# A memset of 128x384 on GpSimd between every two row scatters of a 64-expert routing group

## The reference, cut to what matters

```python
gates = jax.nn.softmax(logits, axis=-1)
w_topk, idx_topk = jax.lax.top_k(gates, TOPK)             # TOPK = 8
...
rank = jnp.arange(A) - starts[se]
valid = rank < CAPACITY                                   # CAPACITY = 160
buf = jnp.zeros((NUM_EXPERTS, CAPACITY, H), x.dtype).at[se, rank].set(x[st], mode='drop')
h = jnp.einsum('ech,efh->ecf', buf, expert_w1)
x1, x2 = jnp.split(h, 2, axis=-1)
out = jnp.einsum('ecf,ehf->ech', x1 * jax.nn.silu(x2), expert_w2)
```

## Time and profile before

| what | us |
|---|---|
| median of three timed runs | 3281.57 |
| lowest and highest of them | 3281.53, 3283.92 |
| span of the profiled execution | 3607.6 |
| TensorE busy in it | 2593.0 (72%) |
| VectorE busy | 2038.9 (57%) |
| GpSimd busy | 1846.4 (51%) |
| ScalarE busy | 1370.6 (38%) |
| scatters of line L1894, stage A | 160, 998 ns each |
| scatters of line L1894, stage B | 128, 977 ns each |

### The profile page before, as it was taken

How to read it: one execution, slowest core, us unless ns; L and a number is a source line. 1 busy time by engine, 2 the same in 40 slices (tenths; PEclk the granted TensorE clock), 3 DMA queues, 4 the chain that set the end, 5 groups by cost and what they waited for, 6 DMA issues and landing times. The chain is left out here.

```text
span 3607.6 us, 68811 instructions
## 1 busy us (share of the span) xinstructions
PE 2593.0 (72%) x24634; PEld 1681.5 (47%) x24634; DVE 2038.9 (57%) x5864; ACT 1370.6 (38%) x2937; POOL 1846.4 (51%) x2072
## 2 busy tenths in 40 slices
PE   1224994735499945689998899947388886999573
PEld 1113884423368834356555555536133332555362
DVE  4347334523443345547885587621699999787413
ACT  1111221301122222344665266622576763466323
POOL 5650775254317742126996213456488886123554
PEclk7666997856599977799999799978699999899786
DMA  9100896121019974331110101112221211111123
GB/s 373 48 1 8 213 224 155 45 66 31 27 41 226 226 191 108 138 120 21 19 19 3 20 19 30 48 55 56 102 94 48 94 62 40 22 20 35 43 80 92
DMA packets 222721, 294.13 MB, mean 82 GB/s; under 512 B 36704, under 2 KB 179583, under 8 KB 216288
## 3 DMA queue, kind: packets, MB, share of 16 engines
q1 hardware_dynamic: 172704, 249.85, 22.3%
q0 software_dynamic: 47616, 39.44, 5.8%
q10 hardware_dynamic: 2112, 1.05, 0.1%
HBM read 181.88 MB, written 107.12 MB: 80 GB/s over the span
## 5 line engine op out<-in xcount | busy, mean ns | idle before, releaser
L3783 POOL TENSOR_TENSOR l3am_db<-l3am_du,l3am_bs 128x1024 f32<-128x1024 f32 x127 | 298.0, 2367 | 39.9 <-DVE l3am_hh L4021 36.1
L4021 DVE TENSOR_TENSOR_SCAN l3am_hh<-l3am_dA,l3am_db 128x1024 f32<-128x1024 f32 x128 | 292.1, 2283 | 0.9 <-ACT l3am_dA L3921 0.7
L1217 POOL TENSOR_TENSOR l2a_pT<-l2a_pT,kept 128x512 int32<-128x512 int32 x213 | 265.1, 1280 | 45.4 <-ACT l2a_pT L1423 45.4
L3066 POOL DMA_INDIRECT l0f_table<-l0f2e_y,l0f2e_idx x128 | 178.9, 1398 | 177.1 <-DVE l0f2e_idx L3038 130.2
L3066 POOL DMA_INDIRECT l0f_table<-l0f1e_y,l0f1e_idx x128 | 179.6, 1403 | 139.2 <-DVE l0f1e_idx L3038 91.2
L4152 PE MATMUL l3am_y<-l3am_hc,ident 128*128 128x512 f32 x512 | 242.1, 596 | 0.0
L3921 ACT ACTIVATE l3am_dA<-l3am_dl,l3am_al 128x512 f32<-128x512 f32 x256 | 166.3, 682 | 130.8 <-DVE l3am_hh L4021 127.2
L1894 POOL DMA_INDIRECT l0f_rows<-l0f1r_row,l0f1r_idx x160 | 159.7, 998 | 103.1 <-issue 69.3
L1304 DVE CUSTOM_DVE_ANT_0 l2a_junk<-l2a_s,addend 128x256 f32<-128x256 f32 x486 | 178.1, 421 | 57.0 <-PE l2a_s L1540 44.6
L1297 DVE TENSOR_REDUCE l3f1a_mx<-l3f1a_s 128x2 f32<-128x512 f32 x243 | 156.5, 685 | 40.9 <-PE l3f1a_s L1540 32.4
L1297 DVE TENSOR_REDUCE l3f2a_mx<-l3f2a_s 128x2 f32<-128x512 f32 x243 | 156.4, 684 | 39.7 <-PE l3f2a_s L1540 32.1
(11 more groups left out here) (848 smaller groups left out, 7045.5 us busy)
## 6 DMA issues: line engine op xcount, KB each, us to landing
l3am_bs<-l3a_b SPq DMA_DIRECT2D x32, 1024.0 KB, 6.6
l0f1m_w<-in_L_ffn_expert_w SPq DMA_DIRECT2D x64, 384.0 KB
l0f2m_w<-in_L_ffn_expert_w SPq DMA_DIRECT2D x64, 384.0 KB
l1a_top<-l1a_kernel SPq DMA_DIRECT2D x16, 1024.0 KB, 12.6
l0f_rows<-blank SPq DMA_DIRECT2D x8, 1930.0 KB, 15.2
l0f1m_w<-in_L_ffn_expert_w SPq DMA_DIRECT2D x64, 192.0 KB
l0f2m_w<-in_L_ffn_expert_w SPq DMA_DIRECT2D x64, 192.0 KB
l3f_rows<-blank SPq DMA_DIRECT2D x8, 1440.0 KB, 11.6
```

Source lines behind the costliest of these rows:

```text
L1217: self.nc.gpsimd.tensor_tensor(t, t, self.kept[:, f // 8 % 2, :].unsqueeze(1).to_broadcast([P, 2, 2 * P]), ALU.mult).then_inc(self.cut_g, 1)
L3066: g.indirect_dma_start(out=tables[p], out_offset=bass.IndirectOffsetOnAxis(ap=idx[u % RING][:, a:a + 1], axis=0), in_=y[u % RING][:, a, :] ...
L3783: G.tensor_tensor(db[n % DB][:, :].rearrange("p (j t) -> p j t", j=CC), du[k % 2][:, :, :], bs[s // QUARTER][:, s % QUARTER, :].unsqueeze( ...
L4021: V.tensor_tensor_scan(hh[n % HH][:, :], dA[n % 2][:, :], db[n % DB][:, :], 0.0, ALU.mult, ALU.add).then_inc(h_ready, 1)
```

## The change

Between every two scatters of a group GpSimd sets a scratch tile of 128x384 floats to zero. A counting semaphore orders the memsets among themselves: each waits until the one before has ended, since they write the same tile. The scatters themselves wait for nothing new. The first scatter of a group has no memset ahead of it, so there are 31 to a group. In a group that is skipped the memsets are skipped too.

```diff
+    PAUSE = 384
...
+        self.pause = ph.sb("pause", [P, self.PAUSE])
...
+        self.paused = ph.sem("paused")
...
         for t in range(TPG):
             for j in range(self.K):
+                if t or j:
+                    k = n * (TPG * self.K - 1) + t * self.K + j - 1
+                    if k:
+                        g.wait_ge(self.paused, k)
+                    self.nc.gpsimd.memset(self.pause[:, :], 0.0).then_inc(self.paused, 1)
                 g.indirect_dma_start(out=self.m.rows, out_offset=bass.IndirectOffsetOnAxis(
                     ap=self.idx[u][:, t, j:j + 1], axis=0), in_=self.row[u][:, t, :], in_offset=None,
                     bounds_check=self.last_slot, oob_is_err=False).then_inc(sent, 16)
```

## The result

The changed kernel takes 3354.61 us (median of four runs, 3347.94 to 3360.22), the kernel before 3281.55 us: the ratio is 1.0221, 95% interval 1.0203 to 1.0239. The change makes it 73 us slower; the forecast was 110 us slower, 3392 us. The profiled execution of the changed kernel has a span of 3358.5 us, 1.7 us under its own time, where that of before had 3607.6 us against a median of 3281.6. So the two profiles differ by 249 us in the other direction than the times. That had to be understood first.

A forecast was written before the change was run, and what follows sets the result against it. GpSimd's string of scatters was taken to end the first routing stage and be about level with the other engines beside the attention; memsets add 64 + 46 = 110 us to 3281.6, giving 3392 us, range 3275 to 3425.

The forecast's parts named there:

- A: First routing stage (l0f1r), five groups of scatters: GpSimd ends it, so 155 memsets at 0.41 us add 64 us.
- B: Stage beside the block attention (l0a), four groups of scatters: 124 memsets add 51 us, of which 46 us count.
- The stall isn't in the runs to be predicted: Both scatter stages: engines stalled during back-to-back scatters mostly in the profiled execution, 326 us longer than the timed median.
- The accounting: Both scatter stages without stall: 108 us and 170 us less, together 278 us, close to the 326 us gap.
- The rest has no room: Outside the two scatter stages: no place for the 326 us, as TensorE is busy 46.5 of 50 us among experts.
- The price of a memset: Between two scatters on GpSimd: 0.14 + 0.41 + 0.16 - 0.30 = 0.41 us each, scatter pitch 1.70 us.
- The slack in B: Beside the block attention: GpSimd ends at 880 us, the other engines at 885, so 5 us of memsets are hidden.
- Rival 1: Both scatter stages: the stall is real in timed runs and memsets relieve it, 168 us faster, 3114 us; chance 0.13.
- Rival 2: Both scatter stages: scatters go out faster unprofiled, 1.0 us each, so some +35 us, 3317 us; chance 0.17.
- Rival 3: Between scatters: the memset runs in the existing gap, 14 us less slack, about 3290 us or no change; chance 0.09.
- Rival 4: Both scatter stages: the stall is real and memsets don't relieve it, 114 us slower, 3396 us; chance 0.09.
- rival 5: At each memset: the semaphore wait costs its high bound, 0.61 us each, 170 us in all, 3445 us; chance 0.07.

The follow-up runs named there:

- experiment 1: The kernel before, unchanged, timed and profiled again: 3281.41 us against 3281.69, ratio 1.0005.
- experiment 2: The changed kernel's memsets put in one stage only: first routing stage 3332.16 us, beside the block attention 3311.45 us, against 3281.69 for the kernel before.
- experiment 5: The changed kernel with memsets of 16 or 1024 elements in place of 384: 3602.99 and 3566.91 us, against 3605.6 for the kernel before on chip 3.
- experiment 9: The changed kernel, no edit, timed on chip 15: 3521.09 us against 3623.79 for the kernel before, ratio 0.9735.
- experiment 7: The changed kernel with 24 scatters that can't keep a row left out of the fifth group: 3321.95 us, ratio 1.0133 to the kernel before.

## Why the prediction was right, and where it wasn't

TensorE's first matmul on expert rows cuts the execution at the ends of A and B. By the tile view, in the kernel before on a stalled chip (first profile), before on a free one, changed on a free one, changed on a stalled one:

```profile
L2961 PE MATMUL l0f1e_x<-ident,l0f1e_row x128: 230/234/396, 354.4 to 578.0; 80*128 80x80 f32 x128
...
L2961 PE MATMUL l0f2e_x<-ident,l0f2e_row x128: 230/234/291, 1058.5 to 1279.4; 80*128 80x80 f32 x128
```
```profile
L2961 PE MATMUL l0f1e_x<-ident,l0f1e_row x128: 230/234/398, 254.5 to 481.4; 80*128 80x80 f32 x128
...
L2961 PE MATMUL l0f2e_x<-ident,l0f2e_row x128: 230/234/292, 802.5 to 1025.5; 80*128 80x80 f32 x128
```
```profile
L2969 PE MATMUL l0f1e_x<-ident,l0f1e_row x128: 230/234/392, 306.6 to 530.2; 80*128 80x80 f32 x128
...
L2969 PE MATMUL l0f2e_x<-ident,l0f2e_row x128: 230/234/396, 874.9 to 1099.0; 80*128 80x80 f32 x128
```
```profile
L2969 PE MATMUL l0f1e_x<-ident,l0f1e_row x128: 230/234/393, 305.1 to 530.6; 80*128 80x80 f32 x128
...
L2969 PE MATMUL l0f2e_x<-ident,l0f2e_row x128: 230/234/397, 960.5 to 1185.7; 80*128 80x80 f32 x128
```

| | to the first experts | from there to the second |
|---|---|---|
| before, stalled | 354.4 | 704.1 |
| before, free | 254.5 | 548.0 |
| changed, free | 306.6 (+52.1) | 568.3 (+20.3) |
| changed, stalled | 305.1 (-49.3) | 655.4 (-48.7) |

**The change on free chips** is 52 + 20 = 72 of the 73 us between the two spans. On stalled ones it is 49 + 49 = 98, for 92 us between the spans of these two profiles, which are of different chips; on chip 15 alone it is the measured 103. The stages behind have next to no part in it.

**The stall isn't in the runs to be predicted: right; that it belongs to the profiled execution: wrong.** "I conclude that the stall belongs mostly to the profiled execution" had the right consequence for the time, since the timed runs came from a free chip, but by all that the runs show the profile and the times were from two kinds of chips. That the sign came out right is luck to this extent: had the timed runs fallen where the profile did, the same change would have been some 100 us faster. The argument for the step was a sum, 278 us of stall against 326 us of difference, and a sum can't tell a profiler from a chip. In every run listed here the span is some 1.7 us shorter than the time of the same execution (3285.1 against 3286.84 in experiment 1). The Trainium skill ("Runtime: NRT & Kernel Launch", The ~15µs preamble/postamble breakdown) says that the profile's total is some 6 us longer than the execution time whatever the kernel; I had set its rule aside because of the 326 us. Its size and its direction aren't those of this case, 1.7 us the other way; its point, that the gap is small and steady, holds here. A gap of 326 us should have led me to look for two machines, not to the profiler.

**The accounting: good where it was worked out, wrong about the rest.** Without the stall A was to end at 241 against VectorE's 226: measured 247.6 and 227.9. The stall was put at 108 us in A and 170 in B: measured 99.9 and 156.1 (table). The 170 took 52.7 - 10.2 for each group, but the steps of the free chip alternate between some 11.7 and 10.2 us, and the groups fall on the longer ones; with 11.7 it is 4 x 41 = 164. "The rest has no room" failed: of the 322.5 us between the two profiles of before, some 70 lie from the first of the two 8-expert stages on. From the first matmul on queries and keys of the first one (L1540) to that of the second passed 3071.9 - 2032.9 = 1039.0 us on the stalled chip and 2786.7 - 1780.6 = 1006.1 on the free one, and from there to the end 535.7 and 498.4 us. Most of it, 31 and 27 us, is lost within the experts of these stages. TensorE's matmuls on the rows of the first, stalled and free (tile view):

```profile
L2961 PE MATMUL l3f1e_x<-ident,l3f1e_row x80: 272/273/447, 2395.0 to 2514.9; 128*128 128x128 f32 x80
```
```profile
L2961 PE MATMUL l3f1e_x<-ident,l3f1e_row x80: 272/273/448, 2131.1 to 2219.9; 128*128 128x128 f32 x80
```

They take 119.9 us in place of 88.8. TensorE is busy 93.0 us of it and 80.9, at a granted clock of 0.88 and 0.96; the rest of the 31 us is idle time. GpSimd sends 80 scatters there (L3058), mostly 1.28 us apart too.

**The price of a memset: 0.41 forecast, 0.30 measured.** The term that failed is the 0.14 us between a scatter and what follows it, from the earlier trace rows: behind a scatter the memset starts at once. The busy time (0.41 against 0.44), the 0.16 us behind it and the wait at no cost were right. 155 x 0.30 = 46 us in A. The other 6 come from longer scatters: their busy time in A is 168.6 us against 163.6 in the undisturbed run of before. Not many more of them are lengthened (13 are over 1.3 us, 11 before), but each by more: up to 1.92 us, for up to 1.77 before. They lie beside wide operations of VectorE. Timeline, changed kernel on the free chip:

```profile
153.81 1.23 DVE L1736 TENSOR_TENSOR l0f1r_big<-l0f1r_big 128x1024 f32<-128x1024 f32 x1
153.97 1.92 POOL L1902 DMA_INDIRECT l0f_rows<-l0f1r_row,l0f1r_idx  x1 [0.17 <-issue]
```

This scatter starts inside such an operation and lasts 1.92 us in place of 0.98. The Trainium skill ("GPSIMD Engine Reference", Key points) says that GpSimd shares its SBUF interfaces with VectorE, with contention where VectorE reads two SBUF inputs. The row agrees. The stalled trace that I had shows only two such scatters in A (1.78 and 1.55 us), and I put them at nothing.

**The slack in B: 5 forecast, 16 by the ends of the engines, 11 by its effect.** The 5 us came from the rough sums 880 and 885. With 0.30 and 11 the sum is 37 - 11 = 26 us in place of 46; 20 to 30 measured (20.3 by the table, 23 and 30 in experiment 2). The forecast with both terms mended, and the 52 measured for A, is 52 + 26 = 78 us, 3360 us. Both terms erred the same way, so the forecast was too high: the measured 3354.6 us lies in the wide range of 3275 to 3425, and 5 us under the forecast's own 3360 to 3410. "So all 64 us count" in A, "nobody waits" for the residual adds, and GpSimd as the end of both stages were right.

**The rivals.** Rival 1 (the stall is real and the memsets relieve it) is true, on another chip than the one that was timed: its 168 us faster became 103, because in B a step at 1.58 us still takes 24.6 us and not 11. Its 3114 us took the gain of a stalled execution off the time of a free one; off 3606 us it would have been 3438. Rival 2 (scatters 1.0 us apart without a profile) is out: 1.28 in every trace. Rival 3 is half true: the gap does take up the first 0.14 us of a memset (experiment 5), but not 0.44. Rival 4 is out by experiment 9, rival 5 by the 1.58 us (its 3445 us doesn't follow from its own 170 us, which give 3452).

## What to carry to other kernels

Before a profile is read, hold its span against the timed runs. If they differ by more than a few us, the profile may show another machine's behaviour, and what it shows as the bound may be absent where the kernel is timed; run the unchanged kernel again, with a profile, on the chip that is timed. A spacer on an engine's queue costs what it goes beyond the gap that is already there, once that engine's string ends the stage; the surest gain is to leave out links of the string (experiment 7, on a free chip), and how much slack a string has includes the landing and the loading behind its last link. The same edit was 73 us slower on one kind of chip and 103 us faster on the other: a verdict on such a spacer holds for the chip that it was timed on.

## What the runs showed of the hardware

Two kinds of chips. On both a scatter is 0.97 to 0.98 us long and bare ones are 1.28 us apart. On the stalled kind GpSimd's back-to-back scatters hold TensorE, VectorE and ScalarE. In B they do it at 1.28 us apart nearly wholly (a step of 10 to 12 us becomes 52 to 53, which is the group's 41 us added); at 1.58 us a step takes 24.6 us, at 2.11 us 13.7; the free kind takes 10 to 13 us at 1.28 and at 1.58. An estimate from these, with 11 us for an undisturbed step: each scatter of B costs the others 1.28, then 1.58 x (1 - 11/24.6) = 0.87, then 2.11 x (1 - 11/13.7) = 0.42 us.

The distance isn't all. Also at 1.28 us apart, a scatter of A costs VectorE (349.1 - 227.9)/160 = 0.76 us, and one of the 8-expert experts costs TensorE (119.9 - 88.8)/80 = 0.39 us. At 1.58 us apart A has no stall (VectorE ends it at 236.5 us, for 234.8 on the free kind), and B has. The scatters of the 64-expert experts, 1.70 us apart and of 80 rows each, don't seem to stall anyone on the stalled kind (46.45 us of TensorE in 50 us; 45.29 in a window of the same stage on the free kind).

The cause isn't settled. The DMA engines aren't busier on the stalled kind (0.22 against 0.33 in the two windows of experiment 1), and the idle time there is put down to "issue", a wait for nothing that the profile shows. What differs between the chips, and whether it goes with the chip or with the core or the session on it, no run tells: chip 9 was free in two sets of runs, and chips 6, 3 and 15 had one each.
